# Set-up of the first heads' score operands: parts split straight from the score buffers, stored part by part

## The reference, cut to what matters

```
xn = layernorm(x)
q, k, v = heads(xn @ wq.T + bq), heads(xn @ wk.T + bk), heads(xn @ wv.T + bv)    # 16 heads of 8
d2 = max(q2[..., :, None] + k2[..., None, :] - 2.0 * qk, 1e-12)
attn = softmax(-sqrt(d2))                       # 4 batches x 16 heads, 1024 x 1024 each
x = x + (attn @ v) @ wo.T + bo + ffn(xn)        # 7 routed experts and a shared one
xn = layernorm(x)
x = x + attention1(xn) + sqrt((xn @ cos(..))**2 + (xn @ sin(..))**2)
```

## Time and profile before

| | us |
|---|---|
| median of 3 runs | 1505.94 |
| the profiled execution, its own time | 1506.58 |
| its span | 1504.9 |
| ACT busy | 1450.2 (96%) |
| DVE busy | 1261.6 (84%) |
| PE busy | 1116.4 (74%) |
| POOL busy | 435.7 (29%) |

### The profile page before, as it was taken

The page is one execution under the profiler, slowest core; times in us unless marked ns, Lnnn a source line. Parts: engine busy times, 40 slices in busy tenths (PEclk is TensorE's granted clock), DMA queues, the critical chain, the costliest instruction groups (busy, mean ns, idle before and its releaser), DMA issues.

```text
span 1504.9 us, 21382 instructions
## 1 busy us (share of the span) xinstructions
PE 1116.4 (74%) x7849; PEld 437.6 (29%) x7876; DVE 1261.6 (84%) x2254; ACT 1450.2 (96%) x798; POOL 435.7 (29%) x314
## 2 busy tenths in 40 slices
PE   4587786887887877878878684776777676675765
PEld 2132222243252441542423311332123122221212
DVE  6987978988989879789797687857898898887986
ACT  3799999999999999999999999999999999999996
POOL 5273460645503302212033220133222133123100
PEclk8598989999999999999999897899999999999999
DMA  4842635223232212122122321051033033030001
GB/s 119 244 128 63 171 114 137 52 56 83 77 133 68 51 42 63 31 55 64 30 67 55 75 64 29 19 151 46 27 124 69 26 111 83 27 111 21 27 27 56
DMA packets 104034, 112.71 MB, mean 75 GB/s; under 512 B 41698, under 2 KB 76002, under 8 KB 103922
## 3 DMA queue, kind: packets, MB, share of 16 engines
q1 hardware_dynamic: 98202, 98.63, 24.1%
q0 software_dynamic: 4464, 11.09, 2.7%
q10 hardware_dynamic: 1256, 1.53, 0.4%
HBM read 66.52 MB, written 44.70 MB: 74 GB/s over the span
## 4 chain that ended last, share of the span: by engine, by line
ACT 66%; DVE 14%; PE 10%; issue 9%; DMA 1%; ACTq 0%; DVEq 0%; SPq 0%
ACT scores L628 23%; ACT scores L617 22%; ACT exp L1144 14%; DVE scores L592 7%; DVE exp L1151 4%; PE pvb L573 3%; ACT exp L1140 3%; PE ring L558 2%; PE ring L1120 2%; ACT ht L878 1%; ACT L628 1%; ACT L617 1%; PE ring L367 1%; PE ring L839 1%; DMA stk<-sum_rows 0%
## 5 line engine op out<-in xcount | busy, mean ns | idle before, releaser
L592 DVE TENSOR_SCALAR scores<-ring 128x1024 f32<-128x1024 f32 x512 | 589.8, 1213 | 27.1 <-PE ring L558 26.3
L628 ACT ACTIVATE scores<-scores 128x8192 f32<-128x8192 f32 x64 | 445.8, 7021 | 0.2
L1144 ACT ACTIVATE exp<-ring 128x1024 f32<-128x1024 f32 x428 | 414.9, 1278 | 7.2 <-PE ring L1120 7.2
L617 ACT ACTIVATE scores<-scores 128x8192 f32<-128x8192 f32 x60 | 417.3, 7021 | 0.7 <-DVE scores L592 0.6
L1120 PE MATMUL ring<-stk 128*128 128x512 bf16 x997 | 302.4, 385 | 141.8 <-ACT exp L1144 108.6
L573 PE MATMUL pvb<-scores,val 128*9 128x256 f32 x4096 | 326.0, 394 | 81.6 <-issue 38.9
L1151 DVE SCALAR_TENSOR_TENSOR exp<-exp 128x512 f32<-128x512 f32 x428 | 329.9, 793 | 61.2 <-ACT exp L1144 56.3
L558 PE MATMUL ring<-stk 64*128 64x512 bf16 x1024 | 209.8, 407 | 63.5 <-DVE scores L592 46.9
L1120 PEld LDWEIGHTS ring<-stk 128*128 128x128 bf16 x1024 | 61.9, 97 | 358.1 <-ACT exp L1144 262.6
L558 PEld LDWEIGHTS ring<-stk 64*128 64x128 bf16 x1024 | 49.8, 93 | 295.7 <-DVE scores L592 207.0
L573 PEld LDWEIGHTS pvb<-scores,val 128*9 128x9 f32 x4096 | 67.2, 89 | 211.9 <-issue 208.2
(11 more groups left out here) (241 smaller groups left out, 1170.3 us busy)
## 6 DMA issues: line engine op xcount, KB each, us to landing
stk<-stack SPq DMA_DIRECT2D x190, 192.0 KB, 2.8
stack<-qp SPq DMA_DIRECT2D x7, 768.0 KB, 4.8
stack<-kp SPq DMA_DIRECT2D x7, 768.0 KB, 3.9
xj<-xg SPq DMA_DIRECT2D x10, 448.0 KB
yg<-yj POOLq DMA_DIRECT2D x10, 448.0 KB
stack<-qp SPq DMA_DIRECT2D x7, 512.0 KB, 5.1
stack<-kp SPq DMA_DIRECT2D x7, 512.0 KB, 4.9
stk<-sum_rows SPq DMA_DIRECT2D x126, 24.0 KB
```

Source lines behind the costliest of these rows:

```text
L592: nc.vector.tensor_scalar(S[place][:, j * N:(j + 1) * N], tile, 1e-12, None, ALU.max).then_inc(o.release(("qk", group, place, j)), 1)
L617: nc.scalar.activation(S[place][:], S[place][:], ACT.Sqrt).then_inc(root_done, 1)
L628: nc.scalar.activation(S[place][:], S[place][:], ACT.Exp, scale=-1.0).then_inc(exp_done, 1)
L1144: nc.scalar.activation(EX[i // 2][:, i % 2, :], tile, ACT.Exp, scale=SCALE1).then_inc(o.release(("qk1", n, i)), 1)
```

## The change

The set-up of batch 0 is rewritten:

- `wq0` and its bias are multiplied by -2 on DVE ahead of the first statistics; the projection then gives -2q itself. The scaling waits for the two matmuls that read the unscaled weights (`gram_half`).
- ACT copies the first half of the turned x when half of it is turned (`turn_half`). k is projected right behind q.
- q's and k's part 0 and squares are taken from the ring by halves of 512 columns, in turns by ACT and DVE; the rests come from the ring in one operation that adds the bias and subtracts part 0 (`scalar_tensor_tensor`). ACT makes part 1 of q, k and the sums. POOL keeps only part 2 of q.
- DVE measures batch 1 (`measure0(chain, 1)`) behind the limits' check instead of behind the branch.
- SP stores each part of the first four heads when it is made. It loads head 0's stack before it branches, and head 1's behind the branch; ACT issues none of these DMAs.
- DVE keeps v and the routes, does all 32 distances of round 0 and turns batch 1 before it branches.
- The other heads' q is stored behind the load of head 1's stack; their v, k and sums behind the load of head 2's. The clearing of `xg` moves from place 1 to place 2 of round 0.
- POOL does two of the three reductions of the angles ahead of `pool_first`.
- `PAIRS` has another order, so that a part's rows can be stored in one DMA on both sides (`PART_ROWS`).

```diff
-PAIRS = [(a, b) for b in range(3) for a in range(3 - b)]
+PAIRS = [(1, 0), (2, 0), (0, 0), (0, 1), (0, 2), (1, 1)]
+PART_ROWS = [[slice(0, 3), slice(3, 6, 2), slice(4, 5)], [slice(2, 5), slice(0, 6, 5), slice(1, 2)]]
...
+        def store_part(sp, dst, side, parts, part, done, lo, hi):
+            sp.dma_start(dst[:, PART_ROWS[side][part], side, :], bcast(parts[lo:hi, part, :], 1, 3 - part)
+                         ).then_inc(done, 16)
...
+            store_rows(Q, qp0, 0, q_heads, 2)
+            store_rows(K, kp0, 0, k_heads, 2)
+            store_rows(Q, qp0, 1, q_half, 1)
+            store_rows(K, kp0, 1, k_half, 1)
+            store_rows(Q, qp0, 2, q_split, 1)
+            store_rows(K, kp0, 2, k_split, 1)
+            sp.wait_ge(ones_stored, 32)
+            sp.wait_ge(sum_heads, 2)
+            sp.wait_ge(sum_half, 1)
+            store_first_sums(slice(0, 2))
+            sp.wait_ge(sump_ready, 1)
+            store_first_sums(slice(2, 3))
...
             act.wait_ge(scaled, 1)
             tile = o.filled(act, ("q0", 0))
-            nc.scalar.activation(qf0[:], tile, ACT.Identity, bias=bq0s, scale=-2.0)
-            nc.scalar.activation(qp0[:, 0, :], tile, ACT.Identity, bias=bq0s, scale=-2.0).then_inc(q_ready, 1)
-            nc.scalar.activation(sq[:], tile, ACT.Square, bias=bq0s, scale=-2.0).then_inc(o.release(("q0", 0)), 1)
-            act.wait_ge(k_ready, 1)
-            nc.scalar.activation(sk[:], kf0[:], ACT.Square).then_inc(sk_ready, 1)
-            act.wait_ge(qr_ready, 1)
+            for cols in HALVES:
+                nc.scalar.activation(qp0[:, 0, cols], tile[:, cols], ACT.Identity, bias=bq0s).then_inc(q_heads, 1)
+            nc.scalar.activation(sq[:, HALVES[1]], tile[:, HALVES[1]], ACT.Square, bias=bq0s).then_inc(squares, 1)
+            act.wait_ge(q_rest, 1)
+            nc.scalar.activation(sq[:, HALVES[0]], tile[:, HALVES[0]], ACT.Square, bias=bq0s).then_inc(squares, 1)
+            tile = o.filled(act, ("k0", 0))
+            nc.scalar.activation(sk[:, HALVES[0]], tile[:, HALVES[0]], ACT.Square, bias=early["bk0"]).then_inc(squares, 1)
+            act.wait_ge(k_heads, 1)
+            nc.scalar.activation(sk[:, HALVES[1]], tile[:, HALVES[1]], ACT.Square, bias=early["bk0"]).then_inc(squares, 1)
+            o.emptied(act, ("q0", 0))
             nc.scalar.activation(qp0[:, 1, :], qf0[:], ACT.Copy).then_inc(q_half, 1)
             tile = o.filled(act, ("sums0", 0))
-            nc.scalar.activation(sump[:, 0, :], tile[0:64, :], ACT.Copy)
-            nc.scalar.activation(sums[:], tile[0:64, :], ACT.Copy).then_inc(o.release(("sums0", 0)), 1)
+            for cols in HALVES:
+                nc.scalar.activation(sump[:, 0, cols], tile[0:64, cols], ACT.Copy).then_inc(sum_heads, 1)
+            o.emptied(act, ("k0", 0))
+            nc.scalar.activation(kp0[:, 1, :], kf0[:], ACT.Copy).then_inc(k_half, 1)
+            o.emptied(act, ("sums0", 0))
+            nc.scalar.activation(sump[:, 1, :], sums[:], ACT.Copy).then_inc(sum_half, 1)
...
+        def load_first_stack(eng, n):
+            eng.wait_ge(zeroed, 2)
+            eng.wait_ge(first_rows, 96)
+            for side in SIDES:
+                load_parts0(eng, n, side, n, stk_in[n])
+            eng.wait_ge(first_sums, 64)
+            for side in SIDES:
+                load_sums0(eng, n, side, n, stk_in[n])
...
+            store_first(sp)
+            load_first_stack(sp, 0)
...
-                store_first(sp)
-                sp.wait_ge(zeroed, 2)
-                sp.wait_ge(ones_stored, 32)
-                sp.wait_ge(first_stored, 128)
-                for n in range(2):
-                    load_half_stack0(sp, n, SIDES[0], n, stk_in[n])
-                store_prepared(sp, o, 0)
-                store_prepared_sums(sp, 0)
+                load_first_stack(sp, 1)
+                store_prepared_q(sp, 0)
...
                         if place == 0 and r == 0:
+                            store_prepared(sp, o, 0)
+                            store_prepared_sums(sp, 0)
+                        if place == 1 and r == 0:
...
+            dve.wait_ge(gram_half, 1)
+            nc.vector.tensor_scalar(early["wq0"], early["wq0"], -2.0, None, ALU.mult)
+            nc.vector.tensor_scalar(bq0s, early["bq0"], -2.0, None, ALU.mult).then_inc(scaled, 1)
             measure0(chain, 0)
```

More of the change, by code:

```diff
@@ L496, in act_first @@
             nc.scalar.activation(rstd[:], mv[:, :, 1], ACT.Sqrt).then_inc(root_first, 1)
-            tile = o.filled(act, ("turn0", 0))
-            for cols in HALVES:
-                cp = nc.scalar.activation(xt0[:, cols], tile[:, cols], ACT.Copy)
-            cp.then_inc(o.release(("turn0", 0)), 1)
+            act.wait_ge(turn_half, 1)
+            tile = o.tiles[o.of[("turn0", 0)][1]]
+            nc.scalar.activation(xt0[:, HALVES[0]], tile[:, HALVES[0]], ACT.Copy)
+            o.filled(act, ("turn0", 0))
@@ L536, in dve_first @@
+            for i, cols in enumerate(HALVES):
+                dve.wait_ge(sum_heads, i + 1)
+                rest = nc.vector.tensor_tensor(sums[:, cols], tile[0:64, cols], sump[:, 0, cols], ALU.subtract)
+            rest.then_inc(o.release(("sums0", 0)), 1)
+            dve.wait_ge(k_half, 1)
+            nc.vector.tensor_tensor(kp0[:, 2, :], kf0[:], kp0[:, 1, :], ALU.subtract).then_inc(k_split, 1)
+            dve.wait_ge(sum_half, 1)
             nc.vector.tensor_tensor(sump[:, 2, :], sums[:], sump[:, 1, :], ALU.subtract).then_inc(sump_ready, 1)
@@ L1424, in _ @@
                     pe.wait_ge(limit_in, 16)
-                nc.tensor.matmul(tile[:, i * P:(i + 1) * P], w, w, start=True, stop=True)
+                mm = nc.tensor.matmul(tile[:, i * P:(i + 1) * P], w, w, start=True, stop=True)
+                if i == 1:
+                    mm.then_inc(gram_half, 1)
             pe.wait_ge(held, 1)
@@ L1429, in _ @@
             pe_turn0(pe, o, 0)
+            pe.wait_ge(scaled, 1)
             pe_project0(pe, o, 0, "q")
+            pe_project0(pe, o, 0, "k")
             tile = o.begin(pe, ("count", 0), AUX)
             pe.wait_ge(held, 2)
-            nc.tensor.matmul(tile[0:1, 0:4], ones_col, within[:], start=True, stop=True).then_inc(ring_full, 1)
-            pe_project0(pe, o, 0, "k")
+            nc.tensor.matmul(tile[0:1, 512:516], ones_col, within[:], start=True, stop=True).then_inc(ring_full, 1)
             pe_sums0(pe, o, 0)
@@ L1800, in _ @@
             count_turns(pool, angle_chain)
+            angle_chain.wait()
+            for size in TWO_PI[:2]:
+                take_turns(pool, angle_chain, size)
             pool_first(pool)
```

163 lines of the change are left out of this document (87 added, 76 removed).

## The result

| | before | after |
|---|---|---|
| median of the runs, us | 1505.67 (6 runs) | 1499.81 (6 runs) |
| ratio of the undisturbed runs | | 0.9957, 95% interval 0.9946 to 0.9969 |
| the same two kernels once more, us | 1505.03 (20 runs) | 1500.09 (7 runs) |
| ratio | | 0.9973, interval 0.9962 to 0.9984 |
| the profiled execution, its own time and span | 1506.58, 1504.9 | 1500.41, 1498.7 |

(One of the first six runs after took 1540.15 at a clock of 0.721; the ratio leaves it out, and the median of the other five is 1499.2.) The kernel became faster: by its ratio 6.5 us in the first comparison and 4.1 in the second, where the medians differ by 4.9. The forecast was 4.3 and the low end of its range 1499.5, so the first result lies just outside the range and the second inside it. The sign and the place were right.

The account below looks back on a forecast made before the run. The prediction took ACT's chain to hang on DVE's first tile and a DVE-bound round 0. Terms -2.3 (split), -2.25 (store and load) and +0.3 (between rounds) gave -4.3 us, 1501.7 us as median; range 1499.5 to 1504.7.

Parts of the forecast that it names:

- What bounds it: Whole kernel: ACT busy 96%, round 0 DVE-bound; an earlier first tile of DVE moves the rest rigidly.
- Head: Set-up's start: scaling held by one POOL memset, 0.85 us, plus 0.35 us of operations; statistics start 1.2 us later.
- The halves of xt: Set-up's head: only ACT's second copy of turned x stays behind the transposes; -0.55 us.
- Split: Set-up's split of q, k and sums: last operation ends at 26.9 instead of 29.15; term one, -2.3 us.
- The sums' store: Behind the split: two small stores land 3.29 us from the second issue, at 30.5; part of term two, -2.25 us.
- The load: Before round 0: second load of sums, issued at 30.9, lands in 3.0 us (bounds 2.8 and 5.06); part of term two.
- Hidden: Before the first tile: DVE's v and routes, PE's and ACT's branches and POOL's angles fit ahead of the load's landing.
- Between the rounds: Between rounds 0 and 1: DVE's branch, 4.22 us, comes back; +0.3 us, taken between 0 and 0.8.
- 1: Set-up: memset holds nothing, sums land in 2.8, branch hidden; 1500.3 us, with shorter hand-overs 1499.5; chance 17%.
- 2: Before or in round 0: second load lands late, 1503.8 us, or head 1's stack is late, 1503.5; chance 16%.
- 3: Round 0: other heads' stores delay a stack and stop DVE; 1506.7 us or slower; chance 7%.
- 4: Whole kernel: no effect, ACT bound by something not tied to DVE's first tile, as x of batch 2; chance 5%.

Follow-up runs that it names:

- e1: Changed kernel with POOL's two memsets of the stack buffers moved behind the angle steps; median 1501.35 us, ratio 0.9973 to the kernel before.
- e3: Changed kernel with the sums stored whole, in two DMAs behind the last split; median 1499.05 us, ratio 0.9966 to the kernel before.
- e7: Kernel before with the new order of PAIRS and SP storing each part of q and k when made; 1505.46 us, ratio 0.9998 to the kernel before.
- e11: Changed kernel with DVE's branch and its measurement of batch 1 in front of round 0 again; 1499.86 us, ratio 0.9970 to the kernel before.
- the repeat: The changed kernel, unedited, timed and profiled once more beside the kernel before; median 1500.09 us, ratio 0.9973.
- e2: Changed kernel with the two scaling operations behind DVE's normalisation of batch 0; median 1501.96 us, ratio 0.9972 to the kernel before.
- e6: Changed kernel with DVE's branch back ahead of round 0's 32 distances; median 1501.20 us, ratio 0.9970 to the kernel before.
- e12: Changed kernel with scaling behind normalisation, DVE's branch ahead of round 0, sums' parts 0 and 1 stored by ACT; 1500.17 us, ratio 0.9973 to the kernel before.
- e8: Kernel before with head 1's stack loaded by SP only when head 0's has landed; median 1505.74 us, ratio 0.9998 to the kernel before.
- e13: Kernel before with head 1's load behind head 0's landing and DVE's batch 1 measurement behind the limits' check; 1505.25 us, ratio 1.0005 to the kernel before.
- e4: Changed kernel with all six row stores held behind k's last split, on SP's queue; median 1505.17 us, ratio 0.9998 to the kernel before.
- e5: Changed kernel with head 0's load behind SP's branch instead of ahead of it; median 1503.81 us, ratio 0.9987 to the kernel before.

## Why the prediction was right in kind and too small in size

- **What bounds it**: right. First tile -6.13, "exp" -6.31; ACT's and DVE's chains moved rigidly.
- **Head**: forecast 1.2 us for the scaling, measured some 0.4 (0.76 later, of which 0.37 is a later landing of `limit_full`, 5.52 against 5.15). I was right that a memset holds the scaling; both do, until 7.31. I was wrong twice: that the hold ends with the memset that is running, and that the statistics must start behind it: they end 0.5 us after the release and would need 1.6. The Trainium skill ("SBUF — State Buffer", section "Who interferes with whom") says that a DVE instruction with one SBUF input outside the two-port modes doesn't contend with GpSimd, which fits; I had priced the queue behind a held instruction as held too. The halves of xt gave 0.4, not 0.55. q's projection: 12.66 for 12.95.
- **Split**: forecast end 26.9, measured 26.46. DVE takes 0.75 for 512 columns with a second operand where I had 0.65, and it did not matter. The hold of k's part 2 behind POOL, which I had put in, does not show: ACT's part 1 of k ended at 24.08 and released it, k's part 2 ran from 24.11, when POOL had 0.03 us left, and took 1.23 us as in the kernel before. In e1, where ACT ended at 23.73, it started at 23.76. Its start is 0.3 us ahead of my 24.4, and that is most of the 0.44.
- **The sums' store**: this is the step that failed, the term of the sum that was mis-sized. I carried over 3.29 "from the second issue on", a row taken right behind 768 KB of row stores, to a setting where most of these had landed. Measured: 1.71; by e3 and e7, 0.55 of the difference is the traffic, the rest the smaller last piece or chance (2.62 in e11). Against my 30.5 the sums were there at 28.79: from the split's end 2.33 us for the 3.59 forecast, so 1.26, three quarters of the error in the first tile (1.61). In the repeat, e1, e2 and e6 too the sums' load was issued by 28.7 to 29.3, where I had 30.5. The split's 0.44 makes up nearly all of the rest. Some of it is luck: from the end of the last split to the first tile I had forecast 7.65 us, the changed kernel took 6.48 and 6.59 in its two traces, and e1, e2, e3, e6, e11 and e12 took 6.58 to 7.46. All are below the forecast, but by 0.2 to 1.2 us, and this trace is the lowest. I had named 2.8 to 5.06 as the bounds for the load and given the store none. The Trainium skill's 2.0 us fixed ("DMA: Bandwidth & Descriptors", "Anatomy of one DMA — SWDGE (gpsimd) path"), which I set aside because of the 3.29, is nearer to 1.71 and to e12's 2.35, but stated for another queue.
- **The load**: forecast 3.0, measured 3.12, and 2.84 to 3.65 in the eight others with head 0's load ahead of the branch. Less of the 5.06 was traffic than I took it for. The last load of sums now goes out 1.2 us behind the first of the rows, before it was 0.4, and this head start is 0.8 of the 1.94 us. From the issue of the rows' load to the landing of the sums it is 5.5 us before, 4.75 to 4.93 in e7, e8 and e13, 4.3 after. What else shortened it stays open: no run takes the head start back alone.
- **Hidden**: right, and more so than I said. DVE idled 4.77 us in front of the first tile; e11 used that room up without harm.
- **Between the rounds**: forecast +0.3. ACT's wait rose from 0.25 to 0.64, and e6 takes it away. Later ACT's small waits for DVE at 306 and 908 us, 0.32 us together in the kernel before, are gone, and 0.2 us more, which I can't assign; so "exp" moved by 6.31 although the first tile moved by 6.13 and this wait grew by 0.4.
- **Rivals**: 1 was the nearest by its number, not by its mechanism: there was a hold, though a cheap one, the branch between the rounds wasn't hidden, and the load took 3.12, not 2.8. Only its shorter hand-overs fit. Its floor of 1499.5 lay just above the first result and below the second. 2 didn't come: head 1's stack was issued at 32.96, behind a branch of 3.5 us on SP (from 29.42), and DVE didn't stop. 3 neither: 252 GB/s on average in the window, and no gap on DVE. 4 neither.

**What carries the gain.** On the chain it is 2.69 us of split and 3.44 us between the split's end and the first tile (9.92 to 6.48). No run takes back the split alone; its 2.69 us are read from the two traces. Of the 3.44 us, 1.27 came with the parts stored as they are made, in one execution of the kernel before with that edit (e7: 8.65 from the split's end to the tile). The rest came with the load of the rows ahead of the landing of the sums, head 1's load moved away, DVE's measurement moved, the sums stored in two steps (0.1 to 1.0, not settled) and chance; e13, with head 1's load and the measurement alone, took 9.41. e4 and e5 name two conditions without which the new order loses 4.2 and 3.3 us, but they take 10.65 and 10.10 us from the split's end to the tile, more than the kernel before, and so aren't shares of its gain. What stays open is the cause of the branches' spread, the share of the rows' own wait, and whether the gain in time is nearer to 4.1 or to 6.5 us.

**What is late next.** In the changed kernel k's third part (stored in 2.5 to 3.0 us) and the sums' third part are tied, and behind both stands the rows' load, with 4.0 to 5.3 us from its issue to the landing of the sums. Moving the split by 0.5 us (e2, e12) moved no tile.

## What to carry to other kernels

A landing time read from a trace belongs to the queue it was read in: when the change takes that queue away, bound it from below as well, by the smallest landing of its size, and give it its own term. Where several conditions meet at one point, list when each is fulfilled before pricing one of them; in the kernel before, the load and DVE's own work were ready within 0.2 us of each other, and removing one of them changed nothing that the time could show. When an experiment takes back one piece of a change, check on the chain that it comes back to the old form: here two of them made a third form that was worse than both. And read small changes in the trace at a point behind the edit and ahead of the noisy part, since two comparisons of the same two kernels differed here by 2.4 us.

## What the runs showed of the hardware

- A taken branch has no fixed price. In front of round 0 it idled DVE for 4.22 us in the kernel before, 4.33 in e8, 2.83 in e7 and 2.08 in e11; behind round 0 for 4.13 to 4.86 (e1, changed); on SP 3.5 and 4.0 (changed, e5). Other engines branching or loading at the same time is a guess that nothing here tested.
- A tensor_scalar with one small column (128 x 1) behind a tensor_scalar was held by POOL's memset just as the 128 x 128 one: rows of 1.39 and 1.53 us, both ending at 7.31.
- The last third of the sums landed in DRAM in 1.71, 2.35 or 2.62 us (changed, e12, e11), the same two stores each time (in e12 with the sums' first parts on ACT's queue), issued 1.4 to 1.7 us behind the last row store: one reading of such a store is good to half a microsecond or worse.
- ACT's waits for PE in layer 1 vary from 6.7 to 12.0 us between executions of kernels that are the same there. The two longest (12.0 in e2, 9.4 in e5) came with a granted clock of 0.97 over 1010 to 1120 us, but so did 8.0 in e7.
